# Conditioned residual block on one core: a new order for the second and third group's tanh and exp, whole first loads, a product moved to GpSimd

## What is computed

```python
# step 1, per batch, prompt type 0, 1 or 2
attn_in = tanh(x @ W1 + b1)                 # 128 x 128
scores = attn_in @ v                        # 128
mask = prefix (l <= j), postfix (l >= j) or cloze (l != j), by the type
p = softmax(where(mask, scores, -1e30))     # 128 x 128
x = x + (p @ x) / count_of_mask
# step 2, per batch, a category out of 64
x = x + (x @ W[cat] + b[cat])
```

## Time and profile before

| | us |
|---|---|
| three runs | 323.30, 323.19, 321.76; median 323.19 |
| the profiled execution, own time | 322.09 |
| its span, first to last instruction | 320.3 |
| busy in the span: PE, DVE, ACT, POOL | 311.7, 283.8, 274.4, 3.6 |
| DMA moved | 101.49 MB, mean 317 GB/s |

### The profile page before, as it was taken

The page is one execution under the profiler, slowest core; times in us unless marked ns, Lnnn a source line. Parts: engine busy times, 40 slices in busy tenths (PEclk is TensorE's granted clock), DMA queues, the critical chain, the costliest instruction groups (busy, mean ns, idle before and its releaser), DMA issues.

```text
span 320.3 us, 4751 instructions
## 1 busy us (share of the span) xinstructions
PE 311.7 (97%) x1374; PEld 242.3 (76%) x1374; DVE 283.8 (89%) x300; ACT 274.4 (86%) x447; POOL 3.6 (1%) x17
## 2 busy tenths in 40 slices
PE   8999897999999999999999999999999999999996
PEld 4445675878888887887888788888878888787884
DVE  3558799999999999999999999999999999999950
ACT  2376988979989899998989999898998989899852
POOL 3010000000000000000000000000000000000000
PEclk9999997999999999999999999999999999999999
DMA  7999999899989989998999999898899989974123
GB/s 227 429 356 422 421 382 335 303 354 308 356 308 345 353 300 381 303 376 299 358 322 320 351 328 368 313 350 317 307 405 297 360 311 353 334 282 178 37 96 131
DMA packets 21290, 101.49 MB, mean 317 GB/s; under 512 B 2385, under 2 KB 2386, under 8 KB 11282
## 3 DMA queue, kind: packets, MB, share of 16 engines
q1 hardware_dynamic: 20882, 100.15, 85.2%
q10 hardware_dynamic: 288, 0.79, 0.7%
q0 software_dynamic: 96, 0.26, 0.3%
HBM read 84.41 MB, written 16.78 MB: 316 GB/s over the span
## 4 chain that ended last, share of the span: by engine, by line
PE 91%; ACT 3%; DVE 2%; DMA 2%; issue 1%; SPq 0%; DVEq 0%; ACTq 0%
PE ps_y L564 17%; PE ps_y L565 16%; PE ps_y L566 16%; PE ps_pre L520 11%; PE ps_y L579 4%; PE ps_y L552 4%; PE ps_y L576 4%; PE ps_y L577 4%; PE ps_y L578 4%; PE ps_pre L509 2%; PE ps_pT L543 2%; DMA x_raw<-in_x 2%; PE ps_scores L530 1%; DVE w_lo L378 1%; PE ps_scores L532 1%; ACT w_hi L261 1%
## 5 line engine op out<-in xcount | busy, mean ns | idle before, releaser
L378 DVE TENSOR_TENSOR w_lo<-w_raw,w_hi 128x2048 fp32r<-128x2048 f32 x60 | 137.1, 2285 | 4.0 <-ACT w_hi L261 4.0
L261 ACT ACTIVATE w_hi<-w_raw 128x2048 fp32r<-128x2048 f32 x60 | 115.9, 1933 | 1.5 <-DVE w_raw L366 1.5
L564 PE MATMUL ps_y<-w_hi,xT_hi 128*128 128x512 f32 x240 | 96.6, 403 | 0.3 <-DVE w_lo L378 0.3
L566 PE MATMUL ps_y<-w_hi,xT_lo 128*128 128x512 f32 x240 | 94.4, 394 | 0.0
L565 PE MATMUL ps_y<-w_lo,xT_hi 128*128 128x512 f32 x240 | 94.4, 393 | 0.0
L566 PEld LDWEIGHTS ps_y<-w_hi,xT_lo 128*128 128x128 f32 x240 | 45.3, 189 | 10.0
L564 PEld LDWEIGHTS ps_y<-w_hi,xT_hi 128*128 128x128 f32 x240 | 45.4, 189 | 9.6 <-ACT out_sb L303 0.5
L565 PEld LDWEIGHTS ps_y<-w_lo,xT_hi 128*128 128x128 f32 x240 | 45.4, 189 | 9.3
L405 DVE TENSOR_TENSOR z_lo<-ps_y,z_hi 128x512 fp32r<-128x512 f32 x64 | 43.5, 682 | 6.3 <-ACT z_hi L297 6.3
L297 ACT ACTIVATE z_hi<-ps_y 128x512 fp32r<-128x512 f32 x64 | 39.0, 610 | 9.3 <-PE ps_y L566 4.8
L366 DVE TENSOR_TENSOR w_raw<-w_raw,ident 128x512 f32<-128x512 f32 x63 | 42.8, 681 | 0.6 <-DMA w_raw<-in_L_cond_W 0.6
(11 more groups left out here) (71 smaller groups left out, 284.5 us busy)
## 6 DMA issues: line engine op xcount, KB each, us to landing
w_raw<-in_L_cond_W SPq DMA_DIRECT2D x63, 1024.0 KB, 8.3
out<-out_sb SPq DMA_DIRECT2D x64, 256.0 KB, 5.4
x_raw<-in_x SPq DMA_DIRECT2D x15, 1024.0 KB, 7.1
w_raw<-in_L_cond_W SPq DMA_DIRECT2D x2, 512.0 KB, 6.6
x_raw<-in_x ACTq DMA_DIRECT2D x1, 512.0 KB, 5.9
x_raw<-in_x SPq DMA_DIRECT2D x1, 512.0 KB, 5.2
w_pack<-in_W_b_v ACTq DMA_DIRECT2D x1, 257.0 KB, 3.2
b_raw<-in_L_cond_b POOLq DMA_DIRECT2D x2, 128.0 KB, 7.2
```

The source lines that it names most:

```text
L261: nc.scalar.activation(w_hi[k % NH][:], w_raw[k % NW][:], ACT.Copy).then_inc(w_hi_ready, 1)
L378: nc.vector.tensor_tensor(w_lo[k % NL][:], w_raw[k % NW][:], w_hi[k % NH][:].bitcast(F32), ALU.subtract).then_inc(w_lo_ready, 1)
L564: nc.tensor.matmul(y[:], xT_hi[q][:, c, xs], w_hi[k % NH][:, c, :], start=(c == 0), stop=False)
L566: last = nc.tensor.matmul(y[:], xT_lo[q][:, c, xs], w_hi[k % NH][:, c, :], start=False, stop=(c == DC - 1))
```

## The change

- The first loads. SP issues x of group 0 as one transfer and nothing before it. ACT issues the ids, the packed W1, and, once the ids are there, the first W as one transfer on its own queue. The extra semaphores of the halves are gone; PE waits for all of x, and for one `add_identity(0)` on the whole W.
- `warm_up` behind the ids' product has 7 products instead of 11.
- The bias table is loaded by SP behind W of batch 4.
- row_div, the product of row sums and counts, is made on GpSimd for all 16 groups; DVE keeps the reciprocal.
- ACT's and DVE's lists for the second and third group are written in another order, and both loops begin at k = 7.
- DVE makes `seen`, `cat_high` and `one_hot` ahead of the first identity.

```diff
@@ the loads: sync
-            sp.dma_start(ids_row[:], ids.rearrange("(a n) -> a n", a=1)).then_inc(ids_in, 16)
-            sp.dma_start(x_raw[0][:, halves[0], :], xg[0][:, halves[0], :]).then_inc(x0_in[0], 16)
+            load_x(0)
             sp.wait_ge(ids_in, 16)
-            cat_0 = sp.value_load(ids_row[0:1, 0:1], min_val=0, max_val=C - 1)
-            for h, c in enumerate(halves):
-                sp.dma_start(w_raw[0][:, c, :], w[bass.ds(cat_0, 1), :, c, :].rearrange("a p c h -> p (a c) h"))\
-                    .then_inc(w0_in[h], 16)
             load_w(1)
             load_w(2)
             load_x(1)
             load_w(3)
             load_w(4)
+            sp.dma_start(b_raw[0:C, :], bias).then_inc(b_low_in, 16)
+            sp.dma_start(b_raw[C:P, :], bias).then_inc(b_high_in, 16)
             load_w(5)
             load_x(2)
             load_w(6)
@@ gpsimd, behind its constants
-            pool.wait_ge(w_in[2], 16)
-            pool.dma_start(b_raw[0:C, :], bias).then_inc(b_low_in, 16)
-            pool.dma_start(b_raw[C:P, :], bias).then_inc(b_high_in, 16)
+            pool.wait_ge(seen_ready, 1)
+            for g in range(GROUPS):
+                pool.wait_ge(exp_ready, g + 1)
+                if g >= 1:
+                    pool.wait_ge(scale_ready, g)
+                nc.gpsimd.tensor_tensor(row_div[:], row_sum[:], seen[:, G * g:G * (g + 1)], ALU.mult)\
+                    .then_inc(div_ready, 1)
@@ scalar
+            act.dma_start(ids_row[:], ids.rearrange("(a n) -> a n", a=1)).then_inc(ids_in, 16)
             act.dma_start(w1_pack[:], w1).then_inc(w1_in, 16)
-            act.dma_start(x_raw[0][:, halves[1], :], xg[0][:, halves[1], :]).then_inc(x0_in[1], 16)
+            act.wait_ge(ids_in, 16)
+            cat_0 = act.value_load(ids_row[0:1, 0:1], min_val=0, max_val=C - 1)
+            act.dma_start(w_raw[0][:], w[bass.ds(cat_0, 1)].rearrange("a p c h -> p (a c) h")).then_inc(w_in[0], 16)
@@
+            split_w_hi(4)
             tanh_group(1)
-            split_w_hi(4)
-            split_z_hi(3)
             split_w_hi(5)
             exp_group(1)
+            split_z_hi(3)
             copy_out(0)
             scale_group(1)
-            copy_out(1)
             split_xT_hi(2)
             split_w_hi(6)
+            split_z_hi(4)
+            split_mix_hi(1)
+            copy_out(1)
             split_w_hi(7)
-
-            for k in range(G + 1, B + 3):
+            copy_out(2)
+            split_z_hi(5)
+            tanh_group(2)
+            split_w_hi(8)
+            copy_out(3)
+            split_w_hi(9)
+
+            for k in range(G + 3, B + 3):
@@ vector
             def row_scale_group(g):
-                dve.wait_ge(exp_ready, g + 1)
-                nc.vector.tensor_tensor(row_div[:], row_sum[:], seen[:, G * g:G * (g + 1)], ALU.mult)\
-                    .then_inc(div_ready, 1)
                 dve.wait_ge(div_ready, g + 1)
@@
-            add_identity_0(0)
-            add_identity_0(1)
@@
-            split_av_lo(0)
             dve.wait_ge(setup_step, 4)
             nc.vector.scalar_tensor_tensor(one_hot[:], cat_all, row_f[:, 2:3], cat_high[:],
                                            ALU.is_equal, ALU.add).then_inc(bias_ready, 1)
+            add_identity(0)
+            split_av_lo(0)
             add_identity(1)
             max_group(0)
             add_identity(2)
-            dve.wait_ge(seen_ready, 1)
             row_scale_group(0)
@@
+            split_w_lo(4)
             split_av_lo(1)
             add_identity(5)
-            split_w_lo(4)
             max_group(1)
+            split_w_lo(5)
+            row_scale_group(1)
             split_z_lo(2)
             split_z_lo(3)
-            row_scale_group(1)
-            split_w_lo(5)
             add_identity(6)
             add_identity(7)
             split_xT_lo(2)
@@
             split_z_lo(4)
             add_identity(8)
             split_w_lo(7)
+            split_av_lo(2)
             add_identity(9)
-
-            for k in range(G + 2, B + 1):
+            split_z_lo(5)
+            split_w_lo(8)
+            add_identity(10)
+
+            for k in range(G + 3, B + 1):
@@ tensor
             def hidden_raw(g):
...
+                pe.wait_ge(x_in[g], 16)
                 for c in range(DC):
-                    if g == 0 and c % HALF == 0:
-                        pe.wait_ge(x0_in[c // HALF], 16)
@@
             def xw_raw(k):
                 for c in range(DC):
-                    if k == 0 and c % HALF == 0:
-                        pe.wait_ge(wi_ready, c // HALF + 1)
-                    elif k >= 1 and c == 0:
+                    if c == 0:
                         pe.wait_ge(wi_ready, wi_count(k))
@@
-            warm_up(11)
+            warm_up(7)
             hidden_raw(0)
```

More of the change, by code:

```diff
@@ L39, in program @@
     assert A == P and w1.shape[1] == DC * A + 2 and D == DC * P and C == P // 2
-    HALF = DC // 2
     NX, NT, NW, NH, NL, NZ, NO, NY = 3, 2, 5, 4, 3, 3, 4, 5
@@ L116, in program @@
         b_high_in = sem("b_high_in")
-        x0_in = [sem(f"x0_in{h}") for h in range(2)]
-        w0_in = [sem(f"w0_in{h}") for h in range(2)]
         x_in = [sem(f"x_in{i}") for i in range(NX)]
@@ L159, in program @@
         block = ctx.enter_context(nc.Block())
-        halves = [slice(h * HALF, (h + 1) * HALF) for h in range(2)]
         def w_count(k):
@@ L166, in wi_count @@
         def wi_count(k):
-            return k + 2
+            return k + 1
         @block.sync
@@ L251, in split_xT_hi @@
             def split_xT_hi(g):
-                act.wait_ge(x_in[g % NX], 16 * (g // NX + (1 if g % NX else 0)))
+                act.wait_ge(x_in[g % NX], 16 * (g // NX + 1))
                 if g > NT:
@@ L357, in diagonal @@
                 return w_raw[slot][:].rearrange("p c (i j) -> p (c i) j", j=P)[:, ::DC + 1, :]
[L359 to L362, removed]
             def add_identity(k):
-                dve.wait_ge(w_in[k % NW], 16 * (k // NW + (1 if k % NW else 0)))
+                dve.wait_ge(w_in[k % NW], 16 * (k // NW + 1))
                 nc.vector.tensor_tensor(diagonal(k % NW), diagonal(k % NW), eye.to_broadcast([P, DC, P]), ALU.add)\
@@ L504, in hidden_raw @@
                     pe.wait_ge(attn_ready, g)
-                    pe.wait_ge(x_in[g], 16)
+                pe.wait_ge(x_in[g], 16)
                 for c in range(DC):
-                    if g == 0 and c % HALF == 0:
-                        pe.wait_ge(x0_in[c // HALF], 16)
                     last = nc.tensor.matmul(ps_pre[:], w1_pack[:, c * A:(c + 1) * A], x_raw[g][:, c, :],
```

## The result

The changed kernel takes 323.12 us (median of 20 runs, 322.55 to 324.52). The kernel before, run beside it on the same chip, takes 321.87 (20 runs, 320.54 to 323.3). The ratio is 1.0037, with an interval of 1.0023 to 1.0051: slower by 0.37%, or 1.2 us. I had forecast 1.6 us saved. The time lies inside the range I gave and the difference under the 0.5% that I called no change, but the sign is the other one, so the forecast was wrong.

A forecast was written before the change was run, and what follows sets the result against it. It took a loop over VectorE and ScalarE, 18.76 us per group, to set the later pace, not PE. 2.54 + 0.17 - 0.9 - 0.2 gave 1.6 us saved, forecast 321.0 us, range 319.0 to 323.5.

The forecast's parts named there:

- The bound: Later groups: a loop over VectorE and ScalarE sets the 18.76 us pace; the end follows neg_max of group four, not PE's gaps.
- The sum. 1: From neg_max of the second group to that of the fourth: 38.04 us instead of 40.58, saving 2.54 us.
- 2: Start of the second group's neg_max in the new order: 30.92 against 31.09 us, nothing gained or lost (-0.17).
- 3: the start, d: First loads: waiting for whole x and whole first W delays the start by d = 0.9 us, ends -0.1 and 4.1.
- The rule that I had set against the edit: Start: DMA engines alternate between queues, so W on ACT's queue would halve x's pace; d nearer 1.9, sum 1.0 us smaller.
- 4: GpSimd's product, p: row_div on GpSimd: 0.2 us later than on VectorE, counted once in the first group, hidden later; bounds 0 and 0.6.
- 5: the rest, at nothing: Bias table on SP's queue, ids on ACT's queue, W1 pack 0.4 us later, and kernel end: no cost.
- A (a late front): Start: x lands at 8.3 or later, first products at low clock; d 1.9 to 4.1, 321.5 to 324.8 us; chance 0.20.
- B: Every group: GpSimd's product comes so late that VectorE waits at the reciprocal; 4 us, 325 us and up; chance 0.05.
- C: Start comes earlier, x in by 6.4: d 0 or less, 2.5 us or more saved, 319.6 us; chance 0.15.
- D: The loop takes the gain back, for example waiting for W of batch 7 or 8; within 1 us of before; chance 0.10.

The follow-up runs named there:

- e4: The kernel before with one swap in ACT's loop: xT_hi of the next group ahead of the copy of a finished batch; 321.5 us, ratio 0.9979.
- e8: e7 with xT_hi of the next group also moved ahead of the copy in ACT's loop; 319.28 us, ratio 0.9912 to the kernel before.
- e7: e3 with the identity of batch 5 moved ahead of w_lo of batch 4 on VectorE; 320.62 us, ratio 0.9954 to the kernel before.
- e2: The kernel before with the new loads alone (x and first W whole, ids and W on ACT's queue, 7 warm-up products); 323.2 us, ratio 1.0047.
- e6: The changed kernel with the first W, whole, on SP's queue between x and W of batch 1; 322.19 us, ratio 0.9996 to the kernel before.
- e5: The changed kernel with 11 warm-up products instead of 7; 323.33 us, ratio 1.0053 to the kernel before.
- e9: The changed kernel with row_div back on VectorE; 322.88 us, ratio 1.0038 to the kernel before.
- e1: The changed kernel with the loads of before (halves of x and first W, ids on SP, 11 warm-up products); 321.34 us, ratio 0.9987 to the kernel before.
- e3: The kernel before with the new order of ACT and DVE alone; loads, row_div and bias table as before; 320.81 us, ratio 0.9962.
- e10: e8 with whole first loads: SP issues ids, x, first W, W of batch 1; ACT W1 alone; 8 warm-up products; 319.42 us, ratio 0.9904.

## Why the prediction was wrong

**The bound** held in one half. The end moved by what neg_max of the fourth group moved: +0.36 us in the trace, +0.3 in the span, and the pace stayed at 18.75. e4 and e8 show the same from the other side. The other half, "and not by PE's gaps", failed for that very instruction: its row carries a wait of 0.73 us for PE, which the low clock had made late. The two engines' loop sets the later turns; before, PE set this one.

**"The sum. 1"** failed at its first term, 6.21 us from neg_max to xT_lo; it was 7.32. I took the distance from neg_max to exp, 0.72, from the earlier trace rows, that is from a turn in which ScalarE is free when neg_max comes. In the new order w_hi of batch 5 stands ahead of exp, and it waits for an identity that the same change had put behind w_lo and av_lo. Both facts stand in the order of the two engines printed ahead; I had listed two identities as hidden work of VectorE and had not asked who waited for the one of batch 5. e7 moves that one instruction and gets 6.33. The other terms after the change came out to 0.01 us. The gain was 1.42 us instead of 2.54. Its other side was mis-sized too: the 40.58 us of before held 1.05 us of low clock, which e2 does without in the same order. Against an execution at full clock the new order gains 39.53 - 39.16 = 0.37 us.

**"2"** held but for a remainder: the new chain to neg_max of the second group was put at 0.17 us shorter, and the distance between the first two neg_max grew from 16.28 to 16.41, where 16.31 was forecast.

**"3: the start, d"** was mis-sized: 0.9 forecast, 2.05 measured at the first product with W, of which 1.65 arrive at the first neg_max. I let x set d, with 7.05 for its last byte, and W as before. x was in by 5.1 us, W at 11.2. The rule that I had set against the edit was applied to the wrong transfer. It was not x that W slowed down but the next W that slowed the first. The rule of the Trainium skill, "DMA: Bandwidth & Descriptors", Queues, rings and completion order, that an engine takes turns between queues with work, agrees with the DMA view: 51.2% and 50.0%, and W at 11.2 instead of 9.1 in e6. The d of 1.9 that I had worked out by it was near, with the wrong reason. The four warm-up products don't explain the loss: e5 has them back and is as slow.

**"4: GpSimd's product, p"** held: 0.2 forecast, nothing measurable in e9. **"5: the rest, at nothing"** holds in the changed kernel, but only since its start is late: in e1 ScalarE stood for the bias table, and the step costs about 0.2 us there. I had set ScalarE's need at 26 us; it comes at 24.

**The base.** I put 321.0 between the sum against the profiled execution (320.5) and that against a median of three runs (321.6). Over twenty runs the median is 1.3 us lower. With the measured d and the measured second group the sum reads -1.6 + 0.85 + 1.11 = +0.36 us, the shift seen at the fourth neg_max. The medians differ by 1.25 us. Most of the 0.9 in between can be the low clock: it was in the profiled execution of before, in about half of the others, and in 3 of 20 of the changed kernel. Against an execution of before at full clock I estimate 1.65 of start + 0.13 up to the second neg_max - 0.37 = 1.4 us lost. 1.25 lies between 0.36 and 1.4. The exact share is open, since a start also differs from one execution to another, below.

**The rivals.** A (a late front) is nearest, by half: d lies in its range of 1.9 to 4.1, but x was early, not late, and the slow matmuls appear in e3 with before's loads as well. I had put its turning point at d over 2.5; since the order gave 1.1 us less than counted, it lay near 1.4. Two errors of about 1 us with one sign, the start and the identity of batch 5, in places that I had priced as independent, and a base with the low clock in it made the loss. B, C and D did not happen.

## What to carry to other kernels

Before a distance from a settled turn is used for a turn in a new order, go through what stands in front of each link on its engine, and ask of each instruction there what it waits for: the one that waits for the other engine is the new link. Put the first loads into one queue in the order of need. Here the first W, on a queue of its own, shared the engines with what the other queue sent next, though that was needed much later. Take the base from as many runs as the effect asks for; three runs were off by as much as the whole change. And look whether the profiled execution is a typical one: here its granted clock, 0.994, was that of nearly half of the runs, and the gain was worked out against it.

## What the hardware showed unexpectedly

**A slow GpSimd beside a two-input VectorE instruction.** All sixteen products, after, by the group of their line (duration min/median/max in ns), and two of them in GpSimd's timeline, one alone and one beside w_lo:

```profile
L243 POOL TENSOR_TENSOR row_div<-row_sum,seen x16: 198/642/913, 18.8 to 299.4; 128x4 f32<-128x4 f32 x16
```

```profile
18.84 0.20 POOL L243 TENSOR_TENSOR row_div<-row_sum,seen 128x4 f32<-128x4 f32 x1 [15.65 <-ACT probs L273]
35.92 0.91 POOL L243 TENSOR_TENSOR row_div<-row_sum,seen 128x4 f32<-128x4 f32 x1 [16.88 <-ACT probs L273]
```

The second ends at 36.83, when w_lo (34.48 + 2.29 = 36.77) is over. The Trainium skill, "SBUF — State Buffer", Who interferes with whom, says that a VectorE instruction with two SBUF inputs and a GpSimd instruction that reads SBUF exclude each other, and the trace agrees. Here it costs nothing, since the reciprocal stands behind w_lo in any case.

**The clock column says 1.00 where PE works at half pace.** In the start after, the weight loads between the x matmuls, one per matmul, first 0.85 us apart and then 0.43:

```profile
8.13 0.34 PEld L509 LDWEIGHTS ps_pre<-x_raw,w_pack 128*128 128x128 f32 x1 [0.52 <-issue]
...
8.98 0.34 PEld L509 LDWEIGHTS ps_pre<-x_raw,w_pack 128*128 128x128 f32 x1 [0.52 <-issue]
...
10.21 0.19 PEld L509 LDWEIGHTS ps_pre<-x_raw,w_pack 128*128 128x128 f32 x1 [0.24 <-issue]
10.63 0.19 PEld L509 LDWEIGHTS ps_pre<-x_raw,w_pack 128*128 128x128 f32 x1 [0.24 <-issue]
```

Half the pace is the lower of the two levels, 1.2 GHz, yet the stretch up to 13.81 us shows a granted clock of 1.00: before the clock first rises the column can't be relied on, and the pace must be read instead. That rise came at about 6.5 us in the profile of before, and near 10 in e3, whose loads and eleven warm-up products are the same; the difference, 5.43 against 3.67 us for the eight matmuls, is 1.76 us that no edit made. The number of warm-up products may add to it. In the seven profiled executions with eleven of them the eight matmuls took 3.67 to 5.43 us, in the five with seven or eight 5.38 to 5.92. One profile each can't settle it: no run has e6's loads with eleven products. So the 0.9% of e8 and e10 holds for a mixture of early and late rises.

**W1 behind x.** W1 was issued 0.56 us behind x, on the other queue, and took 4.9 us to land instead of 3.2. From 1.5 to 5.1 us, when x was in, ScalarE's queue had 2.3% of the engines' time and SP's 81.3%; from 5.1 to 5.7 it had all of it. That is not taking turns. In e6, issued in the same way, it took 5.1 us; where it was issued first on its queue, as in e10, 2.8 us. No run tells why.
